# G's mix beside K's and V's, chunks reordered, and group norm's root moved off GpSimd

## The reference

```python
shifted = jnp.pad(h, ((0, 0), (1, 0), (0, 0)))[:, :T_]
delta = shifted - h
x_lerp = h + delta * x_proj_mu
x0 = jnp.tanh(x_lerp @ xl_w1.T) @ xl_w2.T + xl_b2
x1 = jnp.tanh(x0).reshape(B_, T_, 5, R)
mus = jnp.einsum('btnr,hnr->btnh', x1, x_out_w.reshape(H_, 5, R)) + x_bias
r, k, v, g = ((h + delta * mu) @ w.T for each of four)       # r_mu, k_mu, v_mu, g_mu
w = jnp.tanh((h + delta * w_mu) @ w_w1.T) @ w_w2.T + w_b
wd = jnp.exp(-jnp.exp(w))
# per head: S = S * wd_t + k_t v_t ; o_t = r_t S + (r_t . bonus . k_t) v_t
o = ((o - mean) * lax.rsqrt(var + EPS))                       # group norm, 32 values a group
o = (o * gn_weight + gn_bias) * jax.nn.silu(g)
x = _layernorm(h + o @ o_w.T)
# then: router picks 2 of 16 experts, shared expert + routed experts, layernorm(x + ffn)
```

## Time and profile before

| | |
|---|---|
| three runs | 846.95 us median (846.54 to 847.4) |
| profiled execution | 840.05 us, span of its instructions 838.2 us |
| busy in the span | PE 773.3, POOL 545.6, DVE 532.9, ACT 479.6 us |
| POOL root L1008 | 16 times, mean 2932 ns |
| PE granted clock | 0.986 of full speed over the span |

### The profile page before, as it was taken

How to read it: one execution, slowest core, us unless ns; L and a number is a source line. 1 busy time by engine, 2 the same in 40 slices (tenths; PEclk the granted TensorE clock), 3 DMA queues, 4 the chain that set the end, 5 groups by cost and what they waited for, 6 DMA issues and landing times.

```text
span 838.2 us, 27821 instructions
## 1 busy us (share of the span) xinstructions
PE 773.3 (92%) x8906; PEld 588.8 (70%) x8907; DVE 532.9 (64%) x1714; ACT 479.6 (57%) x1250; POOL 545.6 (65%) x678
## 2 busy tenths in 40 slices
PE   9999999999999999999977759999999999999994
PEld 6666656665566655665555439999999999989741
DVE  4548797777877787678764525555555555555366
ACT  3456666666566655665554305655665665656456
POOL 5565688888888888788886642455554555545444
PEclk9999999999999999999999989999999999999998
DMA  5001111221122202220114512222222222221094
GB/s 175 14 29 43 46 50 38 56 69 49 34 60 65 63 25 60 62 61 26 47 37 128 184 50 72 77 72 62 70 64 61 72 63 60 68 59 44 21 403 189
DMA packets 48271, 61.40 MB, mean 73 GB/s; under 512 B 8594, under 2 KB 33432, under 8 KB 48048
## 3 DMA queue, kind: packets, MB, share of 16 engines
q1 hardware_dynamic: 39200, 42.83, 17.3%
q0 software_dynamic: 8704, 17.06, 6.0%
q10 hardware_dynamic: 272, 0.26, 0.1%
HBM read 37.73 MB, written 23.43 MB: 73 GB/s over the span
## 4 chain that ended last, share of the span: by engine, by line
PE 68%; POOL 13%; issue 9%; ACT 3%; DVE 3%; another core or an unknown queue 2%; SPq 1%; DMA 0%; POOLq 0%; ACTq 0%; DVEq 0%
PE psB L630 16%; PE psO L642 15%; PE psO L559 5%; POOL w_ring L1001 5%; PE psP L342 5%; POOL dispatched_rows L1021 4%; PE psB L501 3%; PE psO L347 2%; PE psP L423 2%; PE psB L491 2%; PE psB L479 2%; PE psP L429 2%; PE psP L619 2%; PE psP L333 2%
## 5 line engine op out<-in xcount | busy, mean ns | idle before, releaser
L1044 POOL DMA_INDIRECT expert_results<-yw_all,row_tail x144 | 147.7, 1026 | 151.8 <-ACT yw_all L914 120.5
L904 ACT ACTIVATE hide<-psB,w_ring 128x128 f32<-128x128 f32 x432 | 126.7, 365 | 85.0 <-DVE hide L1375 44.1
L1021 POOL DMA_INDIRECT dispatched_rows<-rows,slot x128 | 131.0, 1023 | 35.6 <-issue 31.4
L630 PE MATMUL psB<-x1T,w_ring 128*128 128x128 f32 x1152 | 142.3, 277 | 5.2 <-issue 4.6
L642 PE MATMUL psO<-w_sb,hide 128*128 x1152 | 142.6, 277 | 0.5 <-ACT hide L904 0.4
L630 PEld LDWEIGHTS psB<-x1T,w_ring 128*128 128x128 f32 x1152 | 134.2, 192 | 8.6 <-issue 7.9
L642 PEld LDWEIGHTS psO<-w_sb,hide 128*128 128x128 f32 x1152 | 134.2, 192 | 1.0 <-issue 0.9
L1001 POOL TENSOR_TENSOR w_ring<-w_ring,tot 128x128 f32<-128x128 f32 (+2 forms) x160 | 117.6, 754 | 0.0
L1365 DVE COPY w_ring<-w_sb 128x516 f32 x144 | 56.5, 434 | 81.2 <-issue 81.2
L1096 DVE SCALAR_TENSOR_TENSOR psP<-psP,cols,delta 128x512 f32<-128x512 f32 x80 | 57.3, 753 | 54.5 <-PE psP L342 54.5
L863 ACT ACTIVATE hide<-psO,cols 128x512 f32<-128x512 f32 x64 | 44.1, 689 | 62.8 <-PE psO L559 59.3
(11 more groups left out here) (204 smaller groups left out, 1381.4 us busy)
## 6 DMA issues: line engine op xcount, KB each, us to landing
rows<-dispatched_rows SPq DMA_DIRECT2D x144, 66.0 KB
w_sb<-expert_results SPq DMA_DIRECT2D x5, 1024.0 KB, 10.5
h_res<-in_hidden SPq DMA_DIRECT2D x16, 256.0 KB, 3.0
out<-w_sb SPq DMA_DIRECT2D x16, 256.0 KB, 3.4
hT<-in_hidden_t SPq DMA_DIRECT2D x15, 256.0 KB, 4.0
w_sb<-in_w SPq DMA_DIRECT2D x14, 256.0 KB
expert_results<-yw_all,row_tail POOLq DMA_INDIRECT x144
w_sb<-in_w SPq DMA_DIRECT2D x2, 1032.0 KB
```

Of the source, the lines that this page charges most:

```text
L630: last = mm(up_ps(p)[:, c // 2, at:at + PART], w1b[w][s][:, c * 128:(c + 1) * 128], xTe[p][:, s * PART:(s + 1) * PART], start=True, stop=True)
L904: last = A(hide[p][:, c, s * PART:(s + 1) * PART], psB[:, 2 * p + c // 2, at:at + PART], ACT.Relu, bias=w1b[w][s][:, HIDDEN + c:HIDDEN + c ...
L1021: G.indirect_dma_start(rows_dram[:, :], bass.IndirectOffsetOnAxis(slot[u % 2][:, j, k:k + 1], 0), rows[k][u % 2][:, j, :], None).then_inc( ...
L1044: G.indirect_dma_start(back_dram[:, :], bass.IndirectOffsetOnAxis(row_tail[:, i, s, 1:2].bitcast(u32), 0), yw[i][:, s, :], None, bounds_ch ...
```

## The change

Two edits, in one kernel.

First, G's mix gets a bank of its own, bank 0 of `psB`, which the transposes of K have used just before. It is issued right behind K's and V's, in `a_mix_k_v_g`, after a wait for `k_tok` (ScalarE has read the transposes). On TensorE the transposes (`b_k_tok`) go ahead of `b_o_near`, `f_up` 1 ahead of `b_kv`, and `c_place` and `f_up` 2 change places with `a_k` and `a_v`.

Second, group norm's 1/sqrt: VectorE adds a reciprocal behind the sum, ScalarE takes the square root, and GpSimd no longer takes part. A root needs another table of functions on ScalarE than tanh and exp; behind the root a tanh of one column (`warm`) is issued, so that the table goes back at once. `c_sq` moves ahead of `f_hid` 3 on ScalarE and `c_var` from the head of VectorE's list to just ahead of the multiplications for W and R, in the same round as the unit's output.

```diff
+        mix_ps = {MIX_W: P0, MIX_R: P1, MIX_K: P0, MIX_V: P1, MIX_G: psB[:, 0, :]}
...
-            def a_mix_k_v(u):
+            def a_mix_k_v_g(u):
                 done(pe, "exp_w", u)
                 done(pe, "r_done", u)
                 pe.nop(nofuse=True)
-                mix(P0, MIX_K)
-                mix(P1, MIX_V)
+                mix(MIX_K)
+                mix(MIX_V)
+                before(pe, "k_tok", u)
+                mix(MIX_G)
...
-            def a_mix_g(u):
-                done(pe, f"mixed{MIX_V}", u)
-                mix(P1, MIX_G)
...
                 at(0, f_up, 0)
+                at(2, b_k_tok)
                 at(2, b_o_near)
-                at(2, b_k_tok)
                 at(3, fill, 5)
-                at(3, a_mix_k_v)
+                at(3, a_mix_k_v_g)
+                at(0, f_up, 1)
                 at(2, b_kv)
-                at(0, f_up, 1)
-                at(0, c_place)
                 at(3, fill, 10, 5, 5)
                 at(3, a_k)
-                at(3, a_mix_g)
+                at(0, c_place)
+                at(0, f_up, 2)
                 at(3, a_v)
-                at(0, f_up, 2)
                 at(2, b_o_far)
...
             def c_sq(u):
                 done(act, "o_sb", u)
-                before(act, "o_var", u)
+                if u:
+                    done(act, "o_var", 2 * u - 2)
...
+            def c_rstd(u):
+                done(act, "o_var", 2 * u + 1)
+                before(act, "o_norm", u)
+                act.nop(nofuse=True)
+                A(o_rstd[:, :], o_inv[:, :], ACT.Sqrt).then_inc(sem("o_rstd"))
+                A(warm[:, :], minus_half[:, 0:1], ACT.Tanh)
...
                 at(2, a_adapt0)
+                at(0, c_sq)
                 at(-2, f_hid, 3)
                 at(2, a_adapt1a)
                 at(2, a_adapt1b)
                 at(-1, c_x1)
-                at(0, c_sq)
+                at(0, c_rstd)
                 at(-1, c_x1T)
...
-            def c_o_rstd(u):
-                done(pool, "o_var", u)
-                before(pool, "o_norm", u)
-                pool.nop(nofuse=True)
-                G.tensor_tensor(o_rstd[:, :], o_var[:, :], minus_half[:, :], ALU.pow).then_inc(sem("o_rstd"))
...
-                at(2, c_o_rstd)
...
                 V.tensor_reduce(o_var[:, :], o_sq[:, :, :], AX.X, ALU.add).then_inc(sem("o_var"))
+                done(dve, "o_var", 2 * u)
+                V.reciprocal(o_inv[:, :], o_var[:, :]).then_inc(sem("o_var"))
...
-                at(-1, c_var)
...
                 at(1, b_pair, 1)
+                at(0, c_var)
                 at(2, a_mul, MIX_W)
```

More of the change, by code:

```diff
@@ L39 @@
 MIX_ORDER = [MIX_W, MIX_R, MIX_K, MIX_V, MIX_G]
-MIX_BANK = {MIX_W: 0, MIX_R: 1, MIX_K: 0, MIX_V: 1, MIX_G: 1}
 MIX_BUF = {n: i % 2 for i, n in enumerate(MIX_ORDER)}
@@ L136, in build @@
         o_sq = sb("o_sq", [128, UT // DV, DV + 1])
-        o_var, o_rstd = sb("o_var", [128, UT // DV]), sb("o_rstd", [128, UT // DV])
+        o_var, o_inv, o_rstd = (sb(n, [128, UT // DV]) for n in ("o_var", "o_inv", "o_rstd"))
+        warm = sb("warm", [128, 1])
         z = sb("z", [128, TILES, C])
@@ L141, in build @@
         z_std = sb("z_std", [128, TILES])
-        minus_half = sb("minus_half", [128, UT // DV])
+        minus_half = sb("minus_half", [128, TILES])
         z_rstd, z_shift = sb("z_rstd", [128, TILES]), sb("z_shift", [128, TILES])
@@ L334, in by_seq, with mix @@
                 return i
-            def mix(ps, n):
+            def mix(n):
                 if n < 4:
@@ L341, in mix @@
                 kw = {"tile_position": (96, 0)} if n == 3 else {}
-                mm(ps, w, a, start=True, stop=True, **kw).then_inc(sem(f"mix_ps{n}"))
+                mm(mix_ps[n], w, a, start=True, stop=True, **kw).then_inc(sem(f"mix_ps{n}"))
             def fill(u, *n):
@@ L383, in a_mix_w_r @@
                 pe.nop(nofuse=True)
-                mix(P0, MIX_W)
-                mix(P1, MIX_R)
+                mix(MIX_W)
+                mix(MIX_R)
             def a_decay_hid(u):
@@ L1094, in a_mul @@
                 dve.nop(nofuse=True)
-                ps = unflat(psP[MIX_BANK[n]])
+                ps = unflat(mix_ps[n])
                 V.scalar_tensor_tensor(ps, ps, col(f"x_bias{n}"), delta[:, :, :], ALU.add, ALU.mult).then_inc(sem(f"mul{n}"))
@@ L1106, in a_add @@
                 dve.nop(nofuse=True)
-                V.tensor_tensor(mixed[MIX_BUF[n]][:, :, :], unflat(psP[MIX_BANK[n]]), hT[u % 2][:, :, 1:T + 1], ALU.add).then_inc(sem(f"mixed{n}"))
+                V.tensor_tensor(mixed[MIX_BUF[n]][:, :, :], unflat(mix_ps[n]), hT[u % 2][:, :, 1:T + 1], ALU.add).then_inc(sem(f"mixed{n}"))
             def a_gate(u):
```

## The result

Before 846.75 us (846.39 to 847.4, 4 runs), after **902.0 us** (889.26 to 905.91, 4 runs): ratio 1.056, interval 1.046 to 1.067. The ratio takes the two quicker of the four runs after (889.26 and 899.57). The forecast of 837.3 was wrong, in size and in sign. What the experiments add: the same changed kernel took 815.0 us on chip 0, against 823.3 for the kernel before there, ratio 0.990 (0.988 to 0.992), and 896.8 on chip 12, ratio 1.058. The record does not name the chip of the first comparison; its times are like those of chip 12. Most of what follows is on why.

What follows compares the result with a forecast made beforehand. Two equally long rings bound it: GpSimd's own and one through K's projection and decay. Savings of 11 x 1.05 = 11.6, less 1.6 lateness, edges -1.2 + 1.8 - 1.0, gave 9.6 us less: 837.3 us, range 828 to 849.

Steps and rivals of the forecast that it cites:

- The order of the steps: In a middle round: transposes 2.38, mixes 3.76, K's copy 7.92, decay 9.63, step 0 9.76 us after level 4 starts.
- the last term: GpSimd from step 0 to the next level 4 on TensorE: 16.60 plus 0.14 us, closing the round at 26.50.
- rival 3: Faster: pauses in GpSimd's 16.60 us go, TensorE decides at 25.7 or a little less; about 825 us; chance 0.10.
- lateness of K: K's copy on ScalarE starting late after K's projection: 0.15 us a round stays, bounded 0 to 1.27; 1.6 in all.
- the root leaves GpSimd: Root's 2.94 us off GpSimd: its own ring falls from 27.55 to 24.6, scatters end near 7.6 into the round, not 10.53.
- Rival 1: Slower: ScalarE's table loads wait until it runs empty, overrunning their gap by 1.72 us a round; about 858 us; chance 0.15.
- root block: On ScalarE between x1 and x1T: two table loads, root and tanh take 2.96 us, fitting 3.37 with 0.41 to spare.
- Rival 2: No difference: K's copy still starts 1.27 us after its projection, round 27.67; 846 to 848 us in all; chance 0.12.
- something else that costs: Slower by another cost, such as a slower partner on GpSimd's and VectorE's ports or a stall at start or end; chance 0.03.
- G's mix at nothing: On TensorE, G's mix beside K's and V's costs next to nothing, saving 1.06 us; cost bounded 0 to 1.06.
- L466's wait: Sign on TensorE: a wait of about 0.36 us for GpSimd ahead of K's transposes, which `o_near` used to cover.
- Rounds of 26.5: Sign: middle rounds of 26.5 us between relus of f_up0, 1.05 less than 27.55.

## Why the prediction was wrong

**The order of the steps was right.** On chip 0, where no signal is late, they can be held against the clock of the forecast, in us behind level 4's start (261.16): transposes 2.40 (forecast 2.38), mixes 3.80 (3.76), K's copy 7.98 (7.92), end of decay 9.70 (9.63), step 0 9.87 (9.76). K's lateness of 1.27 was gone: its copy starts 0.12 after the projection's end. What was off is the last term: from step 0 to level 4 it took 15.75 and not 16.74, so the round is 25.62 and TensorE sets it, which was rival 3's mechanism (25.7). The gain there is 8.2 us, against 9.6 forecast. That nearness is luck in part: the 9.6 were counted from a kernel before with late signals and rounds of 27.55, and there it takes 24 us less.

**What failed is the bound on the lateness.** It is the term "lateness of K", 0.15 us a round, between 0 and 1.27. In the first comparison the mixes started in time (3.79 behind level 4), and step 0 came at 13.08, 3.3 late. The forecast read, in the earlier trace rows, that K's copy starts 1.27 after its projection and relu 1 after an idle time of 1.90, wrote "no row tells what the lateness is", and bounded it from 0 to 1.27 by the rows before. That treats it as a property of K's hand-over. It was one of the scatters, which stood in the earlier trace rows, on another engine, at the same microseconds; and the step "the root leaves GpSimd" moved them by 3 us onto three mixes and a feed-forward group. An unexplained delay may not be bounded by its present size when the change moves what causes it. The early round of the earlier trace rows, at 38 us, has no scatters beside it: the first starts at 101.9, which the trace would have told. A second term was at nothing without a word: what the wait does to TensorE's clock, 1.5 us of TensorE's time in the round shown.

**The account.** The round in the trace is 26.50 as forecast, 3.32 for the mixes' signals and 1.42 between step 0 and level 4: 31.24. Two things lie in the 1.42, and no run separates them: the stretch at 1.2 GHz, by which the output's matmuls start 1.99 us behind step 0 where it is 0.33 on chip 0, and the second pair of scatters, beside which the output's signal comes 1.56 us late (ScalarE waits 3.90). Against the trace before the profiled execution is 65.9 us longer. The relus of the first group place this: the second comes 1.6 later (108.72 and 110.34); the eleven rounds behind it take 351.72 us, to 462.06, and took 303.73, to 412.45, which is 48.0; the next two are 4.2 and 7.9 longer; the last 4.1 arise behind the pipeline, and no row here explains them. Two of the eleven rounds take 35.1 us, each with a mean clock of 0.81. The mean, 31.97, is 5.2 over the forecast's own mean of 26.75 (27.65 less 1.05, and 0.15 for K's lateness).

**The rivals.** Rival 1 (table loads overrun) is refuted: root block 281.84 to 284.86 on chip 0, 3.02 us (2.96 forecast), with x1T still waiting 0.74 behind it (0.33 in the first comparison's trace, where the block takes 3.02 too):

```profile
281.84 1.28 ACT L823 ACT_TABLE_LOAD   x1
283.13 0.22 ACT L823 ACTIVATE o_rstd<-o_inv 128x16 f32<-128x16 f32 x1
283.37 1.28 ACT L824 ACT_TABLE_LOAD   x1
284.66 0.20 ACT L824 ACTIVATE warm<-minus_half 128x1 f32<-128x1 f32 x1
285.60 0.60 ACT L853 ACTIVATE x1T<-psO 128x512 f32<-128x512 f32 x1 [0.74 <-PE psO L518]
```

The Trainium skill (ScalarE: Activation LUTs, "What ACT_TABLE_LOAD costs") has 1283 ns and a drain of about 1380 ns a switch; the first number agrees with these rows, the second is not in them. Rival 2 did not come either: K's copy starts 0.12 us behind its projection's end on chip 0 and 0.11 in the first comparison. It had the right kind of fault, a late signal of TensorE, but at K's projection and of 1.27 us, where the mixes' signals were 3.3 late. What came falls under the last rival, "something else that costs", which had 0.03. G's mix at nothing was right: three mixes take 1.13 us together (272.54 to 273.67), as two did. The reciprocal took 0.25 and not 0.17, which nothing waited for.

**Signs named beforehand.** L466's wait (0.29 against 0.36), the three mixes' time and the root block came as said. Rounds of 26.5 and step 0 well behind the last scatter but right behind `decay` did not both: step 0 was behind `decay`, which was 3.3 late.

## What to carry to other kernels

Name the cause of every delay that the sum leans on, or price the case that the change makes it larger: look at what every other engine does in the same microseconds, queues of scatters above all. A wait marked "remote" whose giver ended long before is such a delay; add them up before and after. And where GpSimd issues several indirect DMAs in a row while others wait for TensorE, try over a microsecond of other work between them (1.1 and 1.3 us from end to start were enough here), and time the kernel on more than one chip.

## What was not expected of the hardware

- Chips differ. By its medians the kernel before took 841 to 847 us in the first comparison, twice on chip 12, on chip 10 and on chip 4, and 822 to 823 on chips 6, 0 and 11. Nothing in the runs tells what makes the difference, or whether a chip can change its kind. The changed kernel's ratio is 1.056 and 1.058 on the one kind, 0.990 on the other.
- On the first kind, signals of TensorE come late while GpSimd issues scatters with 0.3 to 0.4 us between them, those of ScalarE, VectorE and GpSimd do not: by the semaphores' records from 100 to 500 us, of 368 of TensorE's 79 were over 0.5 us late after the change (the mixes' up to 3.4, one of the feed-forward's 4.7) and none of 903 of the other three, and none of TensorE's 408 in the same kernel on chip 0. The kernel before has as many, 83 of 377, but only 15 of them are over 1.35 us late, against 67: the change made them later, not more.
- Over the 13 traces with such times, from 100 to 500 us, TensorE has 814 signals that are over 0.5 us late, and 811 of them belong to matmuls that end while GpSimd issues an indirect DMA or within 0.4 us behind it. Of the 2970 signals whose matmuls end elsewhere, 3 are late. On both kinds the scatters take as long (128 in 126.2 us after the change, median 0.96), so GpSimd itself is not slower. Whether the issuing or the transfers that it starts hold the signals, no run separates.
- A wait of TensorE can cost twice: behind a pause (busy 1.73 of 4.00 us) its clock fell to 1.2 GHz for 3.4 us, and what it ran then took up to twice as long (2.01 against 1.04 us).
- The trace cannot say whether the signal is late or the matmul itself. Ends of matmuls are modelled; the Trainium skill (Perfetto Trace Analysis, "Tensor Engine Instruction (MATMUL, LD_WEIGHTS)") says that the end is an estimate and that the semaphore is pushed once PSUM has acknowledged the data. TensorE's own starts show pauses in the same stretch (L478 in the trace of the changed kernel: idle 0.32 and 0.44 among its 32), which would fit either. No run tells them apart.
- A power on GpSimd takes 0.58 us for 128x1, 0.73 for 128x2, 0.88 for 128x3, 1.04 for 128x4 and 2.93 for 128x16.
